# A fused convolution and Fourier-layer kernel: transposes in halves, small preparations at other chunks, one shift per channel, and the sum of X taken by VectorE's addition

## What is computed

```python
x = x + high_pass(x)          # 3x3 weights per point, from a softmax
for j in range(4):
    z = conv3x3(x, Kj)                             # conv1
    z = relu(batchnorm(z, gamma[j], beta[j]))      # mean, variance per channel over 8x64x64
    z = conv3x3T(z, Kj)                            # conv2
    x = x + 0.1 * z
    x = batchnorm(x, gamma[j], beta[j])
    x = ifft2(fft2(x) * t(Lj))                     # t real, per channel and frequency
```

## Time and profile before

| | before |
|---|---|
| median of 3 runs | 707.87 us (706.07 to 709.96) |
| the profiled execution | 706.02 us, its span 704.2 us |
| mean granted clock of TensorE | 0.966 |
| busy: PE, DVE, ACT, POOL | 89%, 72%, 49%, 33% of the span |

### The profile page before, as it was taken

One profiled execution on the slowest core, in us unless ns is written; L12 is line 12 of the kernel. 1 busy time (PEld: TensorE's weight loads), 2 busy tenths in 40 slices (PEclk: granted clock), 3 DMA queues, 4 the chain that ended last, 5 costly groups with the idle time before them and its releaser, 6 DMA issues.

```text
span 704.2 us, 14614 instructions
## 1 busy us (share of the span) xinstructions
PE 626.2 (89%) x5840; PEld 199.9 (28%) x5840; DVE 504.7 (72%) x884; ACT 347.9 (49%) x649; POOL 235.0 (33%) x180
## 2 busy tenths in 40 slices
PE   6698999999999889899998888999988889999883
PEld 4222333323332222223322222233222222323231
DVE  3679888974887885638878865388788653877674
ACT  1466666643993242229932422299324222992232
POOL 0367676870222442202224422022244220222200
PEclk9699999999999999999999999999999999999988
DMA  9995111119400203194002130940021319200044
GB/s 184 183 167 95 32 33 31 31 32 198 116 1 2 62 9 81 43 233 103 1 2 61 31 77 24 227 110 1 2 62 25 79 42 227 57 1 2 0 121 121
DMA packets 44787, 51.22 MB, mean 73 GB/s; under 512 B 36528, under 2 KB 36656, under 8 KB 42672
## 3 DMA queue, kind: packets, MB, share of 16 engines
...
## 4 chain that ended last, share of the span: by engine, by line
PE 56%; DVE 19%; issue 12%; POOL 5%; ACT 3%; DMA 3%; SPq 1%; DVEq 0%; ACTq 0%; POOLq 0%
PE psum L1079 32%; PE psum L1154 6%; POOL X L504 4%; PE psum L1223 4%; PE psum L1297 3%; PE psum L1105 2%; DMA X<-X 2%; DVE spare L987 2%; DVE work L1016 2%; PE psum L1254 2%; PE psum L1142 2%; DVE wts L746 2%; DVE X L956 1%; DVE work L981 1%; ACT X L680 1%
## 5 line engine op out<-in xcount | busy, mean ns | idle before, releaser
L1079 PE MATMUL psum<-X,wts 128*32 128x512 f32 x1536 | 178.2, 609 | 10.6 <-ACT X L694 7.2
L1079 PE MATMUL psum<-Z,wts 128*32 128x512 f32 x1536 | 172.5, 595 | 4.3 <-DVE Z L929 4.3
L494 POOL TENSOR_TENSOR Z<-X 128x512 f32<-128x512 f32 x64 | 81.4, 1295 | 251.8 <-DVE X L956 227.8
L655 ACT ACTIVATE work<-X,small 128x512 bf16<-128x512 f32 x128 | 90.7, 711 | 77.0 <-DVE X L956 76.5
L570 ACT ACTIVATE Z<-psum 128x512 f32<-128x512 f32 x64 | 38.1, 596 | 142.0 <-PE psum L1079 130.9
L504 POOL TENSOR_TENSOR X<-Z 128x1024 f32<-128x1024 f32 x24 | 58.0, 2441 | 118.2 <-DVE Z L998 118.2
L849 DVE BATCH_NORM_STATS2 stats<-Z 128x6 f32<-128x512 f32 x60 | 41.1, 688 | 66.0 <-ACT Z L570 66.0
L1079 PEld LDWEIGHTS psum<-Z,wts 128*32 128x32 f32 x1536 | 50.3, 109 | 122.3 <-issue 114.0
L1079 PEld LDWEIGHTS psum<-X,wts 128*32 128x32 f32 x1536 | 47.1, 111 | 129.3 <-issue 118.3
L633 ACT ACTIVATE Z<-Z,small 128x512 f32<-128x512 f32 (+4 forms) x92 | 80.2, 922 | 5.2 <-DVE small L919 4.7
L956 DVE SCALAR_TENSOR_TENSOR X<-psum,X 128x512 f32<-128x512 f32 x64 | 43.8, 684 | 28.7 <-PE psum L1079 28.1
...
## 6 DMA issues: line engine op xcount, KB each, us to landing
...
```

The lines of the kernel that those rows point to most:

```text
L494: nc.gpsimd.tensor_tensor(rows(Z0, REG, bp, CH * (2 * half + i), CH), low, high, op=op)\
L655: nc.scalar.activation(by_row(rest[:, o:o + N // 2].bitcast(bf16)), xc, what, bias=small[:, 26:27], accum_out=sums[:, NCH * i + c:NCH * i ...
L1079: last = nc.tensor.matmul(out_b[C * r:C * r + C, :], weights[:, o:o + C], rows(src, reg, bp, g, CH, dj - 1), start=(dj == 0), stop=(dj == ...
```

## The change

- VectorE's addition gets an accumulator output (the sum of X), and ScalarE sums only the squares. The shift becomes one per channel: a new step ("norm", j, 0) behind conv2's chunk 1 averages the first chunk's mean over the rows on TensorE, and VectorE copies it out (`common_shift`). With a common shift, norm 2 averages the two raw sums, so `aggregate_x` is one instruction, and the arithmetic on them stands behind the average.
- `turn` is two steps: the first half stands behind the pair's last chunk, the second behind the chunk after. slot0c stands right behind fwdH instead of one chunk later.
- The next kernels' weights are made behind chunk 9 of conv2 (was 13), the taps behind chunk 10 of conv1 (was 6).
- Behind norm 2, the row of X2 on 64 partitions is scaled by VectorE instead of ScalarE, and GpSimd's last mixing waits until two of VectorE's copies are scaled.
- In the last layer the moments, norm 2 and the first two affines stand behind pair 3's slot0c instead of pair 2's; the turn of pair 3 and invW of pair 1 come ahead of them.
- SUMS places ScalarE's squares at other chunks.

```diff
 def layer_steps(j):
     after = {
+        1: [("norm", j, 0)],
-        8: fourier(j, 0, "fwdH"),
-        9: [("slot0c", j, 0)] + fourier(j, 1, "fwdW"),
+        8: fourier(j, 0, "fwdH") + [("slot0c", j, 0)],
+        9: fourier(j, 1, "fwdW"),
...
-        11: fourier(j, 1, "fwdH"),
-        12: [("slot0c", j, 1)] + fourier(j, 0, "invW") + [("back", j, 0, 0), ("back", j, 0, 1)],
+        11: fourier(j, 1, "fwdH") + [("slot0c", j, 1)],
+        12: fourier(j, 0, "invW") + [("back", j, 0, 0), ("back", j, 0, 1)],
...
         steps.append(("conv2", j, c))
+        if c % Q == Q - 1 and c + 1 < NCH:
+            steps.append(("turn", j, c // Q, 0))
         if c and c % Q == 0:
-            steps.append(("turn", j, c // Q - 1))
+            steps.append(("turn", j, c // Q - 1, 1))
...
-    steps += [("affine", j, 0), ("copied", j, 0), ("back", j, 1, 0), ("copied", j, 1), ("back", j, 1, 1), ("copied", j, 2)]
+    steps += [("affine", j, 0), ("copied", j, 0), ("copied", j, 1), ("back", j, 1, 0), ("back", j, 1, 1), ("copied", j, 2)]
...
-        5: fourier(j, 3, "fwdH") + [("affine", j, 2)],
-        6: [("slot0c", j, 3)] + fourier(j, 3, "invH"),
+        5: fourier(j, 3, "fwdH") + [("slot0c", j, 3), ("affine", j, 2)],
+        6: fourier(j, 3, "invH"),
...
 def last_steps(j):
-    steps = fourier(j, 2, "fwdH") + [("slot0c", j, 2), ("moments", j), ("norm", j, 2), ("affine", j, 0), ("turn", j, BP - 1)]
-    steps += fourier(j, 1, "invW") + [("back", j, 1, 0), ("back", j, 1, 1)] + fourier(j, 3, "fwdW") + fourier(j, 2, "invH")
-    steps += [("affine", j, 1)] + fourier(j, 3, "fwdH") + [("slot0c", j, 3)] + fourier(j, 2, "invW")
-    steps += [("back", j, 2, 0), ("back", j, 2, 1)] + fourier(j, 3, "invH") + fourier(j, 3, "invW")
+    steps = fourier(j, 2, "fwdH") + [("slot0c", j, 2), ("turn", j, BP - 1, 0), ("turn", j, BP - 1, 1)] + fourier(j, 1, "invW")
+    steps += [("back", j, 1, 0), ("back", j, 1, 1)] + fourier(j, 3, "fwdW") + fourier(j, 2, "invH")
+    steps += fourier(j, 3, "fwdH") + [("slot0c", j, 3), ("moments", j), ("norm", j, 2), ("affine", j, 0), ("affine", j, 1)]
+    steps += fourier(j, 2, "invW") + [("back", j, 2, 0), ("back", j, 2, 1)] + fourier(j, 3, "invH") + fourier(j, 3, "invW")
...
                 if bp == BP - 1 and i == 1 and j + 1 < DEPTH:
-                    pool.wait_ge(bn_ready, 2 * j + 2)
+                    pool.wait_ge(copy_scaled, 3 * j + 2)
...
             def sum_x(j, c):
...
-                for i, what in enumerate((ACT.Identity, ACT.Square)):
...
-                    nc.scalar.activation(by_row(rest[:, o:o + N // 2].bitcast(bf16)), xc, what, bias=small[:, 26:27],
-                                         accum_out=sums[:, NCH * i + c:NCH * i + c + 1]).then_inc(x_summed, 1)
+                nc.scalar.activation(by_row(rest[:, o:o + N // 2].bitcast(bf16)), xc, ACT.Square, bias=small[:, 26:27],
+                                     accum_out=sums[:, NCH + c:NCH + c + 1]).then_inc(x_summed, 1)
...
             def scale_first(j):
-                    if g == 0:
-                        parts.append((X2, REG2, 0, 1, 2 * C, 128))
...
             def aggregate_x(j):
-                dve.wait_ge(x_summed, 2 * NCH * (j + 1))
-                link(nc.vector.tensor_reduce(small[:, 27:29], sums[:, :].rearrange("p (k c) -> p k c", k=2), op=ALU.add, axis=AX))
...
-                nc.vector.tensor_scalar(small[:, 2:6], cm(C_QUAD, R), S(0), None, ALU.mult).then_inc(moments_in, 1)
+                dve.wait_ge(x_summed, NCH * (j + 1))
+                nc.vector.tensor_reduce(small[:, 27:29], sums[:, :].rearrange("p (k c) -> p k c", k=2), op=ALU.add, axis=AX)\
+                    .then_inc(moments_in, 1)
+
+            def common_shift(j):
+
+                n = NUMBER["norm", j, 0]
+                bk.full(n)
+                nc.vector.tensor_scalar(S(26), bank(n)[:, 0:1], -1.0, None, ALU.mult)
+                nc.vector.tensor_scalar(S(32), bank(n)[:, 0:1], 1.0, None, ALU.mult).then_inc(drained[n % BANKS], 1)
+                bk.result(n)
+                dve.sem_inc(shift_ready, 1)
...
             def scale_and_bias(j, which):
...
+                else:
+                    nc.vector.tensor_scalar(small[:, 30:32], bank(n)[:, 0:2], 1.0 / (NCH * N), None, ALU.mult)\
+                        .then_inc(drained[n % BANKS], 1)
+                    bk.result(n)
+                    step(nc.vector.tensor_scalar(S(29), S(30), S(26), None, ALU.add))
+                    link(nc.vector.scalar_tensor_tensor(S(33), in0=S(30), scalar=-1.0, in1=S(32), op0=ALU.mult, op1=ALU.add))
+                    nc.vector.scalar_tensor_tensor(S(17), in0=S(33), scalar=S(29), in1=S(31), op0=ALU.mult, op1=ALU.add)\
+                        .then_inc(means_spread, 1)
...
             def scale_copy(j, i):
+                if i == 0:
+                    z = rows(X2, REG2, 0, 0, 1, 0, 2 * C, 128)
+                    nc.vector.tensor_scalar(z, z, small[2 * C:128, 12:13], small[2 * C:128, 13:14], ALU.mult, ALU.add)
...
             def add_conv2(j, c):
                 nc.vector.scalar_tensor_tensor(xc, in0=by_row(bank(n)), scalar=STEP, in1=xc, op0=ALU.mult,
-                                               op1=ALU.add).then_inc(drained[n % BANKS], 1)
+                                               op1=ALU.add, accum_out=sums[:, c:c + 1]).then_inc(drained[n % BANKS], 1)
...
-                        elif at[1] == 13 and j + 1 < DEPTH:
+                        elif at[1] == 9 and j + 1 < DEPTH:
                             sum_kernels(j + 1)
                             prepare((0,))
...
                         conv1_stats(*at)
-                        if at[1] == 6:
+                        if at[1] == 10:
                             prepare_taps(j + 1)
...
             def average(j, which):
-                pe.wait_ge(moments_in, 2 * j + which)
+                if which == 0:
+                    pe.wait_ge(shift_in, j + 1)
+                else:
+                    pe.wait_ge(moments_in, 2 * j + which)
+                of = (stats[:, 1:2], small[:, 1:2 + R], small[:, 27:29])[which]
```

More of the change, by code:

```diff
@@ L148, in layer_steps @@
     steps += [("moments", j), ("norm", j, 2)] + quarters("fwdH", j, 2, (2, 3))
-    steps += [("affine", j, 0), ("copied", j, 0), ("back", j, 1, 0), ("copied", j, 1), ("back", j, 1, 1), ("copied", j, 2)]
-    steps += [("scaled", j, 2, 1), ("turn", j, BP - 1), ("weights", j)]
+    steps += [("affine", j, 0), ("copied", j, 0), ("copied", j, 1), ("back", j, 1, 0), ("back", j, 1, 1), ("copied", j, 2)]
+    steps += [("scaled", j, 2, 1), ("turn", j, BP - 1, 0), ("turn", j, BP - 1, 1), ("weights", j)]
     rest = {
@@ L243, in build @@
         stats = sb("stats", NCH * 6)
-        small = sb("small", 32)
+        small = sb("small", 40)
         sums = sb("sums", 2 * NCH)
@@ L618, in root @@
                 act.wait_ge(means_spread, 2 * j + which)
-                nc.scalar.activation(small[:, 23:24], small[:, 17:18], ACT.Sqrt, bias=small[:, 18:19],
-                                     scale=float(R * R)).then_inc(std_ready, 1)
+                eps, many = (18, R * R) if which == 1 else (34, 1)
+                nc.scalar.activation(small[:, 23:24], small[:, 17:18], ACT.Sqrt, bias=small[:, eps:eps + 1],
+                                     scale=float(many)).then_inc(std_ready, 1)
             def norm_relu(bp, g, n):
@@ L884, in _ @@
             S = lambda i: small[:, i:i + 1]
+            step(nc.vector.memset(S(34), BN_EPS))
             def aggregate():
@@ L891, in aggregate_x @@
             def aggregate_x(j):
-                dve.wait_ge(x_summed, 2 * NCH * (j + 1))
-                link(nc.vector.tensor_reduce(small[:, 27:29], sums[:, :].rearrange("p (k c) -> p k c", k=2), op=ALU.add, axis=AX))
-                step(nc.vector.tensor_scalar(S(29), S(27), -1.0 / (NCH * N), None, ALU.mult))
-                link(nc.vector.tensor_scalar(small[:, 30:32], small[:, 27:29], 1.0 / (NCH * N), None, ALU.mult))
-                step(nc.vector.scalar_tensor_tensor(S(1), in0=S(30), scalar=S(29), in1=S(31), op0=ALU.mult, op1=ALU.add))
-                link(nc.vector.tensor_scalar(S(0), S(30), S(26), None, ALU.subtract))
-                nc.vector.tensor_scalar(small[:, 2:6], cm(C_QUAD, R), S(0), None, ALU.mult).then_inc(moments_in, 1)
+                dve.wait_ge(x_summed, NCH * (j + 1))
[8 more added lines that the diff above has]
+                dve.sem_inc(shift_ready, 1)
             def scale_and_bias(j, which):
@@ L904, in scale_and_bias @@
                 bk.full(n)
-                step(nc.vector.bn_stats(small[:, 6:12], bank(n)[:, 1:1 + R]))
-                nc.vector.tensor_scalar(S(18), bank(n)[:, 0:1], BN_EPS, None, ALU.add).then_inc(drained[n % BANKS], 1)
-                dve.wait_ge(link_s, count[0])
-                nc.vector.bn_aggr(small[:, 16:18], small[:, 6:12]).then_inc(means_spread, 1)
-                bk.result(n)
-                dve.wait_ge(means_spread, 2 * j + which)
```

(13 more changed lines are left out.)

35 lines of the change are left out of this document (23 added, 12 removed).

## The result

The changed kernel takes 686.57 us (median of 4 runs, 686.19 to 689.43) against 708.91 (4 runs, 706.07 to 710.92): ratio 0.970, 95% interval 0.965 to 0.974, 3.0% faster. The forecast was 688.5. In a later group of runs the same kernel had a ratio of 0.973 (0.970 to 0.977).

What follows compares the result with a forecast made beforehand. TensorE, 89% busy, was taken as the bound. Three layers gave 15.0 us, clock 2.9 + 2.4, last layer -1.1, norm 1 there 0.06, tail -0.3: 19.0, so 707.87 becomes 688.9, stated as 688.5; range 682 to 698.

Steps and rivals of the forecast that it cites:

- ScalarE's halved sums at nothing: ScalarE sheds 64 activations, 45 us of work; counted as no gain, since no long TensorE pause waits for them.
- The accumulator at +0.1: VectorE's addition with an accumulator output costs 0.1 us more each; bounds 0 and +0.7.
- The rival of a halved throughput: VectorE's addition with accumulator takes twice its time, 0.65 us more; about 704 us in all; chance 0.06.
- conv2, +1.0 a layer: Layers 0 to 2: pauses of 2.26, 0.86 and 0.72 go, new waits and the extra average come; +1.0 us per layer.
- the norm's part: Between conv2 and the next conv1, around norm 2: TensorE's pause shrinks from 2.42 to 2.1 us, +0.3 per layer.
- From conv2 to conv1: TensorE's pause before the next conv1 becomes 2.1 us instead of 2.42, +0.3 per layer; norm 1 gains 0.06.
- conv1, 3.65 a layer: Pair 3's pauses of 1.40 before invH and 2.22 before invW both go, 3.65 us per layer.
- The clock, 2.9 + 2.4: Slow TensorE clock behind pauses: 2.9 us back once behind vanished pauses, 2.4 behind norm 2 (bounds 0 and 5.1).
- The last layer: Its conv2 loses 1.1 us, norm 1 gains 0.06, and the later norm 2 and stores cost 0.3 at the end.
- The tail: End of the last layer: TensorE's saving is lost in SyncE's queue of 36 stores; no gain, -0.3 us for waiting issues.
- the 14.3 of the prediction: Last layer: how much later the stores were to start, relative to chunk 15's start, than at 674.14 before; 14.3 us.
- T + 24.9: Last layer: forecast start of the stores, 24.9 us after T, the start of chunk 15.

Runs made afterwards that it cites:

- the preparations alone: Kernel before with only the next weights moved behind conv2's chunk 9 and the taps behind conv1's chunk 10: 687.62 us, ratio 0.971.

## Why the prediction was right, by its own steps

**ScalarE's halved sums at nothing.** Right: taking them back changed nothing that the runs can tell (0.973 and 0.973).

**The accumulator at +0.1.** Right: 84 ns, a row of its own, as the Trainium skill says in VectorE: DVE Perf Modes, "Two Vector instructions with no wait between them". The rival of a halved throughput falls: the addition's rows are as long as before.

**conv2, +1.0 a layer.** The mechanism was right, the size too small. From conv2 to conv1 the second layer went from 71.0 to 69.2, with the norm's part +1.8 against 1.3. The weights took 0.55 for the pair instead of 1.3, so nothing waited at chunk 10: the 1.3 was twice a median over three places, which says little of any one of them. The wait at chunk 8 was 0.53 instead of 1.15, since the forecast gave VectorE a backlog of 0.7 of which it had some 0.2. The 1.30 at chunk 11 was forecast as 1.2.

**From conv2 to conv1.** The pause fell to 2.34, not 2.1: VectorE's 64-partition copy took 0.35 and the two copies followed one another. Norm 1 gained more than its 0.06: from chunk 12 of conv1 to conv2 it is 16.5 against 16.7. Both are small.

**conv1, 3.65 a layer.** Right. The third layer's stage went from 51.5 to 47.6, both with one slow stretch behind norm 2, which is 3.9. The prediction reckoned both pauses in one chain, TensorE 1.5 earlier and VectorE free in time, and that is how they go. What it left unsaid is that the 3.65 can't be split into a price for each part: the 1.40 counts only once the taps are gone, as the runs with slot0c early and the taps at 6 show (15 us lost in the changed kernel; nothing gained on the kernel before).

**The clock, 2.9 + 2.4.** Right in kind. Both slow stretches behind the vanished pauses went; of three behind norm 2, two stayed (4.47 and 4.23 for 24 matmuls), so 1.7 came back rather than 2.4 (half of 5.1 is 2.55, not 2.4; the slip is small). That the pause causes the slow stretch behind norm 2 is shown by filling it; that the shorter pause of 2.34 would help, as the forecast had it, is not: over all runs it followed 21 of 27 pauses of 2.33 to 2.35 and 7 of 9 of 2.41 or 2.42.

**The last layer.** conv2 there lost 0.7 (forecast 1.1). The tail was forecast as bound by 36 stores with nothing gained; it is bound by them, and lost 1.2 instead of 0.3. Affine 0 started 22.0 behind chunk 15 (forecast 22.5) and the stores 24.4 (24.9), but the row took 18.3 and not 16.5. The stores start 11.3 later relative to chunk 15 than before; the 14.3 of the prediction doesn't follow from its own T + 24.9 and 674.14, which give 11.8, and nothing in its sum hangs on it. The 43.1 of before holds one slow fwdW more than the same code had in the run of the preparations alone (41.6), so against an undisturbed tail the loss is up to 2.8.

Of 20.6 us behind the prologue, 19.0 were forecast: 5.4 of 7.3 from conv2 to conv1 with the clock, 14.9 of 15.3 from conv1 to conv2, and a loss of 1.3 in the last layer that was 1.9. That the sum is so near is in part luck: a gain and a loss were both taken too small. In the medians the gain is 22.3, where 19.4 were forecast. That the preparations alone give the same time was not: the other parts gain 1.4 a layer in conv1, and give it back in conv2 (0.2 to 0.5 a layer), in the last layer (3.4, most of it in the tail), and in a slow stretch more, which differs from one execution to the next. The share of each in the medians stays open to about 2 us, as the prologue alone wanders by 4; what makes it wander wasn't tried.
